# Preparing the next stage's first rows and weights one stage early, in buffers that three stages share, and scaling later rows on ScalarE

## The reference, cut to what matters

```python
# cut; LayerNorm with eps 1e-5, H = 16 heads of 32, context of 64 tokens for each element
h = layer_norm(x, ln1_w, ln1_b)
q, k, v = h @ q_w + q_b, ctx @ k_w + k_b, ctx @ v_w + v_b
p = softmax(q @ k.T / sqrt(32), masked)         # 16 heads
x = x + (p @ v) @ cproj_w + cproj_b
h = layer_norm(x, ln2_w, ln2_b)
x = x + gelu(h @ fc_w + fc_b) @ proj_w + proj_b  # 512 -> 2048 -> 512
```

## Time and profile before

| | |
|---|---|
| time, median of 3 runs | 2779.68 us (2777.37 to 2783.21) |
| the profiled execution, its own time | 2779.15 us |
| its span, first to last instruction | 2777.1 us |
| busy: PE, DVE, ACT, POOL | 95%, 52%, 28%, 14% of the span |
| stage l3 attention | from 2187.3 to 2400.9 us of the span |
| stage l3 MLP | from 2401.8 us to the end |

### The profile page before, as it was taken

One profiled execution on the slowest core, in us unless ns is written; L12 is line 12 of the kernel. 1 busy time (PEld: TensorE's weight loads), 2 busy tenths in 40 slices (PEclk: granted clock), 3 DMA queues, 4 the chain that ended last, 5 costly groups with the idle time before them and its releaser, 6 DMA issues. The chain is left out here.

```text
span 2777.1 us, 30412 instructions
## 1 busy us (share of the span) xinstructions
PE 2638.4 (95%) x12328; PEld 1928.4 (69%) x12328; DVE 1450.3 (52%) x2282; ACT 782.8 (28%) x1363; POOL 392.3 (14%) x282
## 2 busy tenths in 40 slices
PE   9999999999899999989999999979999889799999
PEld 7777778777678888745454444358888656578887
DVE  6466566655764443445445454375343586763443
ACT  4322332233231111215335353431011244321110
POOL 0000000000130000014334243441000310220000
PEclk9999999999899999999999999999999999999999
DMA  4100110110100000222212122120000100100001
GB/s 192 51 35 36 61 61 16 46 61 1 50 16 31 31 0 1 104 77 56 53 40 59 54 49 49 40 110 31 16 16 1 69 1 0 65 13 19 31 1 61
DMA packets 35604, 118.28 MB, mean 43 GB/s; under 512 B 8069, under 2 KB 8198, under 8 KB 25994
## 3 DMA queue, kind: packets, MB, share of 16 engines
q1 hardware_dynamic: 35466, 116.35, 12.7%
HBM read 81.18 MB, written 7.34 MB: 32 GB/s over the span
## 5 line engine op out<-in xcount | busy, mean ns | idle before, releaser
L1607 DVE TENSOR_REDUCE l_top<-l_slot 128x1 f32<-128x512 f32 x256 | 170.8, 680 | 204.2 <-PE l_slot L1409 203.6
L1558 ACT ACTIVATE l_weighed<-l_across 128x512 f32<-128x512 f32 (+1 forms) x320 | 183.7, 595 | 291.0 <-PE l_across L1433 287.6
L389 PE MATMUL l_wide<-l_key_map,l_norm 128*128 128x260 f32 x1024 | 235.2, 383 | 2.7 <-ACT l_norm L544 2.3
L389 PEld LDWEIGHTS l_wide<-l_key_map,l_norm 128*128 128x128 f32 x1024 | 191.7, 190 | 32.1 <-ACT l_norm L544 2.7
L1433 PE MATMUL l_across<-l_q_stack,l_k_stack 99*128 99x512 f32 (+1 forms) x320 | 192.2, 604 | 10.9 <-ACT l_weighed L1558 7.8
L1236 POOL TENSOR_TENSOR l_paired<-l_weighed 128x2048 f32<-128x2048 f32 x32 | 145.6, 4549 | 379.3 <-ACT l_weighed L1558 323.7
L725 DVE TENSOR_TENSOR x<-l_added,x 128x512 f32<-128x512 f32 x128 | 87.1, 688 | 82.0 <-PE l_added L131 60.5
L1433 PEld LDWEIGHTS l_across<-l_q_stack,l_k_stack 99*128 99x128 f32 (+1 forms) x320 | 57.6, 181 | 97.0 <-issue 65.6
L1409 PE MATMUL l_slot<-l_k_stack,l_q_stack 97*128 97x512 f32 x256 | 111.3, 435 | 11.1 <-DMA l_k_stack<-l_k_parts 6.5
L2405 ACT ACTIVATE l3m_hidden<-l3m_up,columns 128x512 f32<-128x512 f32 x64 | 44.2, 692 | 271.1 <-PE l3m_up L131 259.0
L2405 ACT ACTIVATE l2m_hidden<-l2m_up,columns 128x512 f32<-128x512 f32 x64 | 44.2, 693 | 270.4 <-PE l2m_up L131 265.6
(11 more groups left out here) (391 smaller groups left out, 5952.6 us busy)
## 6 DMA issues: line engine op xcount, KB each, us to landing
l_k_stack<-l_k_parts SPq DMA_DIRECT2D x192, 72.0 KB, 2.0
l_q_stack<-l_q_parts SPq DMA_DIRECT2D x192, 64.0 KB, 2.0
l_wk<-in_weights SPq DMA_DIRECT2D x9, 1024.0 KB, 4.8
l_wv<-in_weights SPq DMA_DIRECT2D x9, 1024.0 KB, 4.9
l_wo<-in_weights SPq DMA_DIRECT2D x9, 1024.0 KB, 4.8
l_wqT<-in_weights SPq DMA_DIRECT2D x8, 1024.0 KB, 6.9
l0m_raw<-in_weights SPq DMA_DIRECT2D x8, 1024.0 KB, 4.8
l2m_raw<-in_weights SPq DMA_DIRECT2D x8, 1024.0 KB, 4.9
```

The lines of the kernel that those rows point to most:

```text
L389: last = pe.matmul(wide[:, j, 0:W], norm[:, k, at:at + P], key_map[:, k, b, :, :].rearrange("p h c -> p (h c)"), start=k == 0, stop=k == K ...
L1558: act.activation(weighed[0:height(c), (CHUNKS * g + c) % RING, j, :], across[0:height(c), use % 2, :], ACT.Exp)\
L1607: dve.tensor_reduce(top[:, t, j:j + 1], slot[:, i % 2, :], AX.X, ALU.max, negate=True).then_inc(s["top_ready"], 1)
```

## The change

The three stages named above get a common set of buffers, `Handover`: two raw weight blocks, one high and one low split block, the small tiles for statistics, and the third block's `rows` buffer. In these:

- The l2m stage ends with the statistics, root and scaled rows of element 0 for the attention stage (`next_moments` ahead of the last but one group of DVE's additions to `x`, `next_rows` behind it).
- The attention stage opens with the transposes, without statistics. The key weights are loaded ahead of the query weights, and ACT splits the query weights behind the four `take_norm`s instead of ahead of them. DVE computes, for elements 1 to 3 together, the reciprocal and an offset (minus mean x reciprocal); ACT makes the scaled rows of these elements as Identity with scale and offset (`later_rows`).
- During its last two elements the attention stage does for the MLP stage what it had done for it: statistics and rows of element 0 (DVE and ACT), the load of the first w1 block (SP, once the logits of element 2 are done), and its split by POOL.
- The l3m stage opens with the transposes; the first load is the first block of w2, and the second block of w1 is loaded without a wait.

```diff
+class Handover:
+    def __init__(self, n, rows, mem):
+        self.rows = rows
+        self.raw = n.sbuf("handover_raw", [P, 2, KT, D], F32, mem)
+        self.high, self.low = (n.sbuf(f"handover_{w}", [P, KT, D], F32R, mem) for w in ("high", "low"))
...
+    def moments(self, n, dve, link, ready):
+        for j in range(TPB):
+            link(dve.bn_stats(self.stats[:, j, :], n.x[:, j, :]), j == TPB - 1)
+        for j in range(TPB):
+            link(dve.bn_aggr(self.mean_var[:, j, :], self.stats[:, j, :]), j == TPB - 1)
+        dve.tensor_scalar(self.second[:, :], self.mean_var[:, :, 1], 1e-5, None, ALU.add).then_inc(ready, 1)
+
+    def scale_rows(self, n, dve, link):
+        link(dve.reciprocal(self.spread[:, :], self.deviation[:, :]))
+        for j in range(TPB):
+            dve.tensor_scalar(self.rows[:, j, :], n.x[:, j, :], self.mean_var[:, j, 0:1], self.spread[:, j:j + 1], ALU.subtract, ALU.mult)
...
@@ l3_attention, SP @@
+            sp.dma_start(wk, n.block("l3_wk")).then_inc(s["wk_loaded"], 16)
             sp.dma_start(wq_raw, n.block("l3_wq")).then_inc(s["wq_loaded"], 16)
-            sp.dma_start(wk, n.block("l3_wk")).then_inc(s["wk_loaded"], 16)
...
+            sp.wait_ge(s["logits_done"], (B - 1) * TPB)
+            sp.dma_start(shared.raw[:, 0, :, :], n.block("l3_fc1", 0)).then_inc(s["next_loaded"], 16)
+            sp.wait_ge(s["next_loaded"], 16)
@@ l3_attention, POOL @@
             for b in range(B):
-                pool.wait_ge(s["rows_ready"], b + 1)
+                if b:
+                    pool.wait_ge(s["rows_ready"], b)
...
+            pool.wait_ge(s["next_loaded"], 16)
+            pool.wait_ge(s["work_done"], WORK["query", B - 1, GROUPS - 1] + 1)
+            for k in range(KT):
+                pool.tensor_copy(shared.high[:, k, :], shared.raw[:, 0, k, :]).then_inc(s["next_high"], 1)
+                pool.wait_ge(s["next_high"], k + 1)
+                pool.tensor_tensor(shared.low[:, k, :], shared.raw[:, 0, k, :], shared.high[:, k, :].bitcast(F32), ALU.subtract)
@@ l3_attention, ACT @@
+            def later_rows(b):
+                act.wait_ge(s["offset_ready"], 1)
+                use = ("norm", b - 1, KT - 1)
+                act.wait_ge(s["turned_done"], TURNED[use] + 1)
+                for j in range(TPB):
+                    last = act.activation(rows[:, j, :], n.x[:, b * TPB + j, :], ACT.Identity, bias=offset[:, b, j:j + 1],
+                                          scale=spread[:, b, j:j + 1])
+                last.then_inc(s["rows_ready"], 1)
...
-            roots(0)
+            for k in range(KT):
+                take_norm(0, k)
             act.wait_ge(s["wq_loaded"], 16)
             for k in range(KT):
                 act.copy(wq_hi[:, k, :], wq_raw[:, k, :]).then_inc(s["wq_high"], 1)
-            for k in range(KT):
-                take_norm(0, k)
             for m in range(GROUPS):
                 take_query(0, m)
             for b in range(1, B):
                 roots(b)
+            later_rows(1)
...
+                if b + 2 < B:
+                    later_rows(b + 2)
+                if b == B - 2:
+                    next_roots()
@@ l3_attention, DVE @@
+            def offsets():
+                dve.wait_ge(s["deviation_ready"], B - 1)
+                link(dve.reciprocal(spread[:, 1:B, :], deviation[:, 1:B, :]))
+                dve.scalar_tensor_tensor(offset[:, 1:B, :], mean_var[:, 1:B, :, 0], -1.0, spread[:, 1:B, :], ALU.mult, ALU.mult)\
+                    .then_inc(s["offset_ready"], 1)
...
                 shift(b, 0)
+                if not more:
+                    next_rows()
...
                 normalise(b, 2)
-                if b + 2 < B:
-                    scale_rows(b + 2)
...
                 normalise(b, 3)
+                if b == B - 2:
+                    next_moments()
@@ mlp_stage, SP @@
-            sp.dma_start(raw1[:, :, :], n.block(first, 0)).then_inc(raw1_loaded, 16)
+            if not prepared:
+                sp.dma_start(raw1[:, :, :], n.block(first, 0)).then_inc(raw1_loaded, 16)
@@ mlp_stage, ACT @@
-            roots(0)
+            if not prepared:
+                roots(0)
             turned_out(0)
...
+            if shared is not None and not prepared:
+                act.wait_ge(variance_ready, B + 1)
+                act.activation(shared.deviation[:, :], shared.second[:, :], ACT.Sqrt).then_inc(deviation_ready, 1)
@@ mlp_stage, DVE @@
-            moments(0)
-            scale_rows(0)
+            if not prepared:
+                moments(0)
+                scale_rows(0)
...
+                    if shared is not None and not prepared and f == FB - 1 and c == B - 2:
+                        next_moments()
                     add_downs(f, c)
+                    if shared is not None and not prepared and f == FB - 1 and c == B - 2:
+                        next_rows()
```

110 lines of the change are left out of this document (65 added, 45 removed).

## The result

| | median us (runs) | ratio to before, 95% interval |
|---|---|---|
| before | 2777.03 (18) | |
| changed kernel | 2782.18 (18) | 1.0017 (1.0010 to 1.0023) |
| forecast | 2770.5, range 2766.0 to 2775.5 | |

The kernel became 0.17% slower, some 5 us, where 9 us less were forecast. The difference is within the 0.2% named as the smallest that can be told, but its interval excludes a gain. One of the 18 runs of the changed kernel took 3348 us at a mean granted clock of 0.748; the ratio leaves it out, here and in the experiments such runs are left out of all ratios. The profiled execution of the changed kernel took 2780.6 us, its span is 2778.9.

What follows compares the result with a forecast made beforehand. The prediction took PE, busy 95% of the span, to bound the kernel, so only its idle could be won: 5.1 + 1.5 + 2.4 = 9.0 us off 2779.15, with half a microsecond for the median 2770.5 us, range 2766 to 2775.5.

Steps and rivals of the forecast that it cites:

- The change takes no matmul away: Whole kernel: PE is busy 95% of the span and keeps all its matmuls, so only PE's idle time can be gained.
- the end of l2m: nothing: End of the third block's MLP, forecast with the attention stage's elements 1 to 3: added statistics and rows fit in idle time, gain nothing.
- Opening of the MLP: Start of the fourth block's MLP stage: transposes start at its first instruction; gain 5.1 us, bounds 3.5 and 7.0.
- the sum by the trace: MLP opening: counts the added table load at 1.28 us without a drain, as the trace shows, giving 5.1 us.
- the gain of 3.7: MLP opening by the skill page's 2.66 us a table switch, drain included; whole sum 1.4 us smaller.
- the weak bound: MLP opening: gain only 3.5 us if PE's half products run at the low clock and hold up `turn(1)`.
- Opening of the attention stage: Fourth block's attention: first query product ends earlier, most of the 7.6 us wait not won; gain 1.5 us, bounds 0 and 4.2.
- new idle in the loop behind ACT's rows: Attention stage: PE showing such idle was named as a sign that the whole prediction is wrong.
- End of element 0: Attention stage: PE's 2.44 us idle ahead of the probabilities' transposes goes; gain 2.4 us, weak bound 1.4.
- The two attention terms: Attention stage: gains of 1.5 us at its opening and 2.4 us at the end of element 0.
- Waits only change their owner: Rival, 2774 to 2779 us: query split late, row activations nearer 0.78 us, table load and low clock eat gains; chance 0.22.
- Slower: the clock: Rival, about 2780 us: both new openings bring the low clock into dense work, about 10 us each; chance 0.03.

Runs made afterwards that it cites:

- e1: Changed kernel plus 32 unused bytes at the end of the shared tiles, making the distance a multiple of 256: 2776.11 us, ratio to before 0.9987.
- e2: Kernel before plus 32 unused bytes between rows and weights of all three MLPs: 2789.43 us, ratio 1.0045.
- e8: Changed kernel plus 32 unused bytes ahead of the shared tiles, keeping the changed kernel's distance: 2783.35 us, ratio to before 1.0018.
- e12: Changed kernel plus 32 bytes behind the shared tiles and gaps of 192 and 160 bytes in the first and second block's attention: 2768.56 us, ratio to before 0.9965.
- e4: Changed kernel plus 32 bytes behind the shared tiles, scaled rows of elements 1 to 3 back on DVE: 2773.34 us, ratio to before 0.9987.
- e9: e7 plus gaps of 192 and 160 bytes in the first and second block's attention: 2768.68 us, ratio to before 0.9967.
- e11: e4 plus gaps of 192 and 160 bytes in the first and second block's attention: 2771.16 us, ratio to before 0.9975.
- e10: Kernel before plus unused tiles of 192 and 160 bytes in the first and second block's attention: 2772.57 us, ratio 0.9983.
- e3: Kernel before plus gaps of 64, 96 and 128 bytes between rows and weights in the first, third and fourth block's MLP: 2789.31 us (1 run).
- e5: Kernel before plus gaps of 256, 512 and 1024 bytes between rows and weights in the first, third and fourth block's MLP: 2781.86 us (1 run).
- e7: Changed kernel plus 32 bytes behind the shared tiles, scaled rows of element 1 alone back on DVE: 2773.20 us, ratio to before 0.9976.
- e6: Kernel before, first MLP's rows and weights moved together by 32 bytes, gaps of 192 and 384 in the third and fourth block's MLP: 2779.1 us (1 run).

## Why the prediction was wrong

**"The change takes no matmul away", and so the matmuls' time was taken as fixed: this is the step that failed.** They were as many, but 512 triples of up products got 19 ns longer and 64 of the queries 13: +10.6 us by the triples, where the prediction had a zero, and not even in a stage it called touched: in "the end of l2m: nothing" lies 4.9 us, all along that MLP. e1, e2 and e8 show the cause: the 32 bytes alone make or undo it, with and without the change. As a time they were worth 6 us (medians) to 8.5 (equal clock) between e1 and the changed kernel. The forecast and this term together give 2770.5 + 10.6 = 2781.1; measured 2782.2. That fit is partly luck, as the next points show.

**Opening of the MLP, -5.1 us: right.** Transposes 5.5 us earlier, first up product 5.1, `turn(1)` 4.8 (e12: 5.8), the last down product 4.3 to 5.7 in e1, e4, e9 and e12, and 4.1 in e11. The table load took its 1.28 us with no drain behind it, so the sum by the trace held; the gain of 3.7 by the Trainium skill, page "ScalarE: Activation LUTs", section "What ACT_TABLE_LOAD costs", did not. The rows of element 1 took 4.53 us next to POOL, not 3.88, and yet began when forecast. The first up products did run at a granted clock of 0.50, from 2407.7 to 2411.0, as the weak bound feared; they were over 1 us before `turn(1)` and cost nothing there.

**Opening of the attention stage, -1.5 us: the chain was right at the place it spoke of, the gain there larger, then given back.** The key weights' wait was 3.6 us (forecast about 4), eight key matmuls again 3.78, and the last quarter was released by POOL. The first logits came 2.7 us earlier, because ACT began to split the query weights 12.9 us into the stage and not 14.6. But the transposes of element 1's rows followed the logits by 3.6 us before, and by 7.2 now: at that point the changed kernel is 1.0 us behind. The prediction only asked for DVE to have 1.92 us less ahead of its first `shift`; it did not cost the mask, the three elements' moments and the common offset that now stand there in one chain, nor that they run beside POOL (2.47 us for the mask; 0.97, 1.04 and 0.87 for the three additions of `second`, which before took 0.87, 0.17 and 0.17). It had named "new idle in the loop behind ACT's rows" as what would make it wrong.

**End of element 0, -2.4 us: the idle went, the time did not.** With ACT's rows PE does turn the probabilities without idle, as forecast; with DVE's an "issue" idle of 1.2 to 1.3 us stays (2.4 before, 1.2 to 2.4 in the other kernels without the change). But the moment itself is 71.6 us into the stage before, and 71.9 to 73.5 in every kernel with the preparation. Four row activations took 2.93 us, not 2.7. The two attention terms, -3.9 together, came out as +0.3 to +1.9 at this point. The step that failed is that PE was taken to reach its logits as early as before: it began late at element 1, and the two low stretches of the granted clock behind that wait cost it 3.4 us more (PE busy 27.91 us instead of 24.53; in e1, with one such stretch, 26.24). A low stretch that begins within 2 us of element 1's transposes stands in the traces of all six kernels in which ACT makes rows, and in none of the eight others. By the stage's end the traces spread by 2.5 to 3 us within either kind (before 214.0, e10 211.5; e4 210.2, e12 213.2), more than what is sought. Most of that spread goes with the number of low stretches of 3.4 us behind the opening: with one, 210.6 and 211.0 without the change (e3, e2), 210.2 and 210.7 with it (e4, e1); with three, 214.0 without it (before, e5), 211.6 to 213.2 with it (e7, e9, changed, e12). Two (e10 211.5, e11 212.8) and four (e8 213.6) lie between or above; e6, with 213.3 and one, had another long one in its opening.

**Elements 1 to 3 and the end of l2m: nothing, as forecast, apart from that and from the pace.** DVE's second mixed part is still released by ACT, 0.63 us after DVE was free (1.34 before).

**What is left of the 9 us.** e12 against e10 is the change with all distances right in both: 0.9965 against 0.9983, about 5 us less (medians 4.0, at an equal clock 2.9), of the forecast 9.0. e1 against before gives 3.6 by the ratio and 2.7 at an equal clock. The MLP's opening alone accounts for that; the attention stage's terms should have been near nothing. About 3 less and 8.5 more, both at an equal clock, make 5.5 more; measured are 5.2, at an equal clock 5.8.

**The rivals.** "Waits only change their owner" came closest in mechanism for the attention stage: it had the split of the query weights last and the activations nearer 0.78 (they took 0.73). "Slower: the clock" did not happen in its size or at its places: the mean granted clock is 0.983 in the trace before and 0.985 in the changed kernel's, and the windows in which fewer matmuls lie are at 1.00. Its mechanism did, in the loop: two low stretches behind a new wait, 3.4 us. The cause of most of the slowness, the matmuls' pace, was in no rival.

**Still open.** Why the distance matters, and why a remainder of 192 costs less than one of 32. Rows are read in 2048 bytes and weights in 512 of each partition; two reads that meet somewhere would fit, but no run shows where. Which engine should scale the rows is open at a level of 1 us; ACT for elements 2 and 3 looks better by 0.8 to 2.7. Why the granted clock fell behind element 1's rows in some schedules and not in others is open as well: in e4 and e11 PE waited 2.38 us there and the clock stayed, in e7 and e9 it waited as long and the clock fell.

## What to carry to other kernels

When a change adds, drops or reorders tiles, matmuls it does not touch may change their pace. Compare the count of matmuls in a window in which PE is never idle, and the mean duration of each group, before looking for waits. Here 512-column matmuls on split (fp32r) operands wanted moving and stationary tiles a multiple of 256 bytes apart; small tiles of odd size belong behind the large ones, or get padded.

An idle stretch that disappears is only a gain if the engine was not late when it reached the place, and a new wait of PE can bring a stretch at the low clock behind it, in which dense matmuls start 0.43 us apart instead of 0.23. Runs of one kernel are best compared with their mean granted clock beside them. Price a moved preparation to the next two points where engines meet, not to the first.

## What the runs showed of the hardware, unexpected

- Three successive matmuls of 512 columns in the MLPs, at a granted clock of 1.00, take 680 ns from start to start when the operands' distance in a partition is a multiple of 256 bytes, and 687 to 702 ns (medians) for other remainders. It did not depend on a common shift of both by 32 bytes, nor on whether a tile is shared between stages.
- 32 unused bytes per partition made a kernel 12.5 us slower (e2), or one 6 to 8 us faster (e1 against the changed kernel).
- PE was busy 27.91 us with the matmuls that took it 24.53 before, where the granted clock fell to 0.50 for 3.4 us twice, and 26.24 where it fell once (e1).
- A table load between two activations cost 1.28 us, 2409.69 to 2410.98, with no further gap in front or behind.
- An activation with a scale and an offset from SBUF took 0.73 us for 128x512; a DVE instruction of 128x4 took 1.04 us next to POOL's split and 0.17 elsewhere.
